# Attention scores over row halves of the array, the half-height mix first, and a projection spread over bank 7 and the next pair

## The reference, cut to what matters

```python
h = concat(patch_embedding(x), txt)                  # 8 x 178 x 192
xn = layernorm(layernorm(h)) * ln_w
Q = xn[:, None] * W_qk[None, :, None, :]             # 12 heads; queries are keys
attn = softmax(mask(Q @ Q^T / sqrt(192)))            # 178 x 178, causal
out = (attn @ (xn - mean(wte, axis=0))) / position   # wte: 50257 x 192
h = h + concat_heads(out) @ W_o.T                    # 2304 -> 192
h = h + experts(layernorm(h))                        # 16 experts and a shared one
```

## Time and profile before

| | |
|---|---|
| three runs | 474.68, 474.75, 476.51 us |
| the profiled execution | 476.25 us, its span 474.4 us |
| TensorE busy | 97% of the span |
| VectorE, ScalarE, GpSimd busy | 59%, 37%, 21% |
| attention, first scores to the end of the projections | about 18 to 278 us |
| transfers of wte | 26 to 220 us, at about 214 GB/s |
| TensorE's granted clock, mean | 0.989 |

### The profile page before, as it was taken

How to read it: one execution, slowest core, us unless ns; L and a number is a source line. 1 busy time by engine, 2 the same in 40 slices (tenths; PEclk the granted TensorE clock), 3 DMA queues, 4 the chain that set the end, 5 groups by cost and what they waited for, 6 DMA issues and landing times. The chain is left out here.

```text
span 474.4 us, 7317 instructions
## 1 busy us (share of the span) xinstructions
PE 459.4 (97%) x2692; PEld 397.7 (84%) x2692; DVE 281.9 (59%) x742; ACT 175.8 (37%) x573; POOL 101.8 (21%) x111
## 2 busy tenths in 40 slices
PE   8699999999999999999998999999999999999997
PEld 8387769866699666897766999989999999999996
DVE  7567856367572787507497636697447754754443
ACT  1365467044580555803445035532311231221211
POOL 6013122221223211210014014921170017000000
PEclk9799999999999999999899999999999999999999
DMA  7867999999999999978316023221323232223330
GB/s 206 255 241 138 213 214 211 214 215 212 214 214 213 214 213 213 214 151 213 120 37 240 2 72 69 61 48 65 86 63 61 66 80 61 63 73 72 74 66 25
DMA packets 23685, 64.99 MB, mean 137 GB/s; under 512 B 2876, under 2 KB 13332, under 8 KB 23266
## 3 DMA queue, kind: packets, MB, share of 16 engines
q0 software_dynamic: 7904, 40.86, 41.0%
q1 hardware_dynamic: 14882, 22.68, 17.6%
q10 hardware_dynamic: 864, 1.00, 0.6%
HBM read 61.88 MB, written 1.27 MB: 133 GB/s over the span
## 5 line engine op out<-in xcount | busy, mean ns | idle before, releaser
L513 ACT ACTIVATE pm<-bank,nmax 128x128 f32<-128x128 f32 x96 | 33.9, 365 | 106.0 <-DVE nmax L1011 106.0
L795 PE MATMUL bank<-woT,area_o 128*128 128x192 f32 (+1 forms) x432 | 71.4, 327 | 0.0
L1100 DVE TENSOR_TENSOR area_b<-area_b,area_w 128x356 f32<-128x356 f32 x64 | 33.9, 529 | 62.1 <-ACT area_b L581 62.0
L795 PEld LDWEIGHTS bank<-woT,area_o 128*128 128x128 f32 (+1 forms) x432 | 70.0, 182 | 0.4
L418 POOL DMA_DIRECT2D area_w<-in_L_attn_wte_dram x26 | 31.4, 1227 | 127.2 <-DMA area_w<-in_L_attn_wte_dram 127.2
L876 PE MATMUL bank<-area_w_r,area_o_r 128*128 128x356 f32 x112 | 43.9, 392 | 0.0
L742 PE MATMUL bank<-pT,xn 128*128 128x356 f32 x96 | 38.8, 486 | 1.1 <-issue 0.5
L581 ACT ACTIVATE area_b<-bank,area_k 128x356 f32<-128x356 f32 x32 | 17.8, 557 | 59.2 <-PE bank L880 59.1
L912 PE MATMUL bank<-area_k,area_b 128*128 128x192 f32 (+1 forms) x192 | 36.8, 327 | 0.0
L877 PE MATMUL bank<-area_w_r,area_o_r 128*128 128x356 f32 x112 | 36.4, 325 | 0.0
L539 ACT ACTIVATE area_b<-xb,w 64x192 f32<-64x192 f32 x96 | 34.5, 456 | 0.1
(11 more groups left out here) (219 smaller groups left out, 1012.9 us busy)
## 6 DMA issues: line engine op xcount, KB each, us to landing
area_w<-in_L_attn_wte_dram POOLq DMA_DIRECT2D x28, 1344.0 KB, 12.6
area_w<-gate_rows SPq DMA_DIRECT2D x64, 178.0 KB, 3.0
area_k<-in_experts_dram SPq DMA_DIRECT2D x8, 353.0 KB, 5.3
area_a<-in_experts_dram SPq DMA_DIRECT2D x6, 353.0 KB, 4.9
woT<-in_L_attn_W_o_dram SPq DMA_DIRECT2D x1, 1728.0 KB, 15.4
area_o<-in_x_dram SPq DMA_DIRECT2D x4, 384.0 KB, 9.1
area_w<-area_w POOLq DMA_DIRECT2D x1, 1344.0 KB, 9.8
area_b<-in_experts_dram SPq DMA_DIRECT2D x3, 353.0 KB, 7.0
```

Source lines behind the costliest of these rows:

```text
L513: last = act.activation(pm[:, sl, j, :], bank[0][:, j * P:(j + 1) * P], ACT.Exp, bias=nmax[:, sl, j:j + 1], accum_out=psums[:, sl, j:j + 1])
L795: last = pe.matmul(o, oT[:, c, at:at + n], woT[:, c, :], start=(c == 0), stop=(c == NCH - 1))
L1100: dve.tensor_tensor(sil[:, n % 2, :], sil[:, n % 2, :], wbc[:, m % RING, :], ALU.mult).then_inc(weighted, 1)
```

## The change

- **Scores.** Heads 0, 1 of a unit go to bank 0 and heads 2, 3 to bank 1, each bank holding the 256 columns of two heads and the 178 of their tail tile. The 64-row part is no longer padded: heads 0, 1 use partitions 0 to 63 and heads 2, 3 partitions 64 to 127, so that the two matmuls of such a step use the two row halves of the array and different banks. `xb` is kept twice, once in each half. The order is: 128-row parts of both banks, the masks, then the 64-row parts of the two banks, main and tail.
- **Behind the scores.** `maxima` is four reductions instead of two. The exponentials go bank by bank (two heads and a tail, then the other three); semaphores are one per bank instead of main and tail.
- **Start.** `xb` goes out of the bank twice (a second copy by ScalarE); the clearing of the padding by VectorE and GpSimd (L950, L405) is gone.
- **Mix.** The half-height part (bank 6) comes first, then banks 4 and 5; `mix_out` on VectorE takes bank 6 first.
- **Projection.** In pairs 0 to 2 tile 0 goes to bank 7 instead of bank 4. Tile 2 is left out at the end of the pair and comes in the next pair behind `scores(1)`; its residual moves along. In the last pair all three stay in order.

```diff
...
         emb_bank = [bank[n] for n in (6, 5, 4, 7)]
         in_a = area_a.shape[1] // WX
 
+        def projected(i, t):
+
+            if t == 2:
+                return bank[5][0:TT, 0:E]
+            return bank[7][:, 0:E] if t == 0 and i < PAIRS - 1 else bank[4][:, t * E:(t + 1) * E]
+
         def expert_at(e, plain):
 
             kept, a, b = (area_k, area_a, area_b) if plain else (round_k, round_a, round_b)
...
             pool.wait_ge(pool_own, own.at)
             pool.memset(wts[:], 1.0).then_inc(s_const, 1)
             pool.wait_ge(s_const, 1)
-            pool.memset(qb[64:P], 0.0).then_inc(s_pad, 1)
-            pool.wait_ge(s_pad, 3)
 
             def rstd(n, count):
 
...
 
                 act.wait_ge(xnT_psum, bt + 1)
                 act.activation(xa[:, b, :], bank[7][:, 0:SP], ACT.Copy).then_inc(xnT_ready, 1)
-                act.activation(xb[0:64, b, :], bank[7][0:64, SP:2 * SP], ACT.Copy).then_inc(xnT_ready, 1)
+                act.activation(xb[0:64, b, :], bank[7][0:64, SP:2 * SP], ACT.Copy)
+                act.activation(xb[64:P, b, :], bank[7][0:64, SP:2 * SP], ACT.Copy).then_inc(xnT_ready, 1)
 
             def exps(u, U):
                 sl = u % 2
-                act.wait_ge(max_main, U + 1)
-                for j in range(GRP):
-                    last = act.activation(pm[:, sl, j, :], bank[0][:, j * P:(j + 1) * P], ACT.Exp,
-                                          bias=nmax[:, sl, j:j + 1], accum_out=psums[:, sl, j:j + 1])
-                last.then_inc(exp_main, 1)
-                act.wait_ge(max_tail, U + 1)
                 for k in range(2):
-                    last = act.activation(pt[:, sl, k, :], bank[1][:, k * S:(k + 1) * S], ACT.Exp,
-                                          bias=nmax[:, sl, 4 + k:5 + k], accum_out=psums[:, sl, 4 + k:5 + k])
-                last.then_inc(exp_tail, 1)
+                    act.wait_ge(max_of[k], U + 1)
+                    for j in range(2):
+                        n = 2 * k + j
+                        act.activation(pm[:, sl, n, :], SIDE[k][:, j * P:(j + 1) * P], ACT.Exp,
+                                       bias=nmax[:, sl, n:n + 1], accum_out=psums[:, sl, n:n + 1])
+                    act.activation(pt[:, sl, k, :], SIDE_TAIL[k], ACT.Exp, bias=nmax[:, sl, 4 + k:5 + k],
+                                   accum_out=psums[:, sl, 4 + k:5 + k]).then_inc(exp_of[k], 1)
 
             def prob_out(u, U):
 
...
 
                 for g in groups:
                     for h in range(GRP * g, GRP * g + GRP):
-                        last = act.activation(qb[0:64, b, :, h, :], xb[0:64, b, :].rearrange("p (c t) -> p c t", c=3),
-                                              ACT.Copy, scale=w2b[:, h:h + 1])
+                        side = ROWS[h % GRP // 2]
+                        last = act.activation(qb[side, b, :, h, :], xb[side, b, :].rearrange("p (c t) -> p c t", c=3),
+                                              ACT.Copy, scale=w2b[side, h:h + 1])
                     last.then_inc(qb_ready, 1)
 
             turn_out(0, 0)
...
 
                 g, b = u % UPB, u // UPB
                 h = GRP * g
-                main = bank[0][:, :].rearrange("p (j t) -> p j t", j=GRP)
-                if not isinstance(U, int) or U:
-                    pe.wait_ge(exp_main, U)
-                split = bank[0][:, :].rearrange("p (j c t) -> p j c t", j=GRP, c=2)
-                pe.matmul(split, xa[:, b, 0:P], qa[:, b, 0:2, h:h + GRP, :].rearrange("p c j t -> p j c t"),
-                          start=True, stop=False)
-                pe.matmul(split, xb[:, b, 0:P], qb[:, b, 0:2, h:h + GRP, :].rearrange("p c j t -> p j c t"),
-                          start=False, stop=False)
-                pe.matmul(main, identb[:], cmask[:].rearrange("p (a t) -> p a t", a=1).broadcast_to([P, GRP, P]),
-                          start=False, stop=True).then_inc(scores_main, 1)
-                if not isinstance(U, int) or U:
-                    pe.wait_ge(exp_tail, U)
+                mains = [m.rearrange("p (j t) -> p j t", j=2) for m in SIDE]
+                splits = [m.rearrange("p (j c t) -> p j c t", j=2, c=2) for m in SIDE]
                 for k in range(2):
-                    o = bank[1][:, k * S:(k + 1) * S]
-                    pair_a = qa[:, b, 2, h + 2 * k:h + 2 * k + 2, :].rearrange("p j t -> p (j t)")
-                    pair_b = qb[:, b, 2, h + 2 * k:h + 2 * k + 2, :].rearrange("p j t -> p (j t)")
-                    pe.matmul(o, pair_a, xa[:, b, 0:S], start=(k == 0), stop=False, skip_group_check=True)
-                    pe.matmul(o, pair_b, xb[:, b, 0:S], start=False, stop=(k == 1), skip_group_check=True)
-                o = bank[1][:, 0:2 * S].rearrange("p (j t) -> p j t", j=2)[:, :, P:S]
-                pe.matmul(o, identb[:], tmask[:, 0:TAIL].rearrange("p (a t) -> p a t", a=1).broadcast_to([P, 2, TAIL]),
-                          start=False, stop=True, skip_group_check=True).then_inc(scores_tail, 1)
+                    at = slice(h + 2 * k, h + 2 * k + 2)
+                    if U:
+                        pe.wait_ge(exp_of[k], U)
+                    pe.matmul(splits[k], xa[:, b, 0:P], qa[:, b, 0:2, at, :].rearrange("p c j t -> p j c t"),
+                              start=True, stop=False, skip_group_check=True)
+                    pe.matmul(SIDE_TAIL[k], qa[:, b, 2, at, :].rearrange("p j t -> p (j t)"), xa[:, b, 0:S],
+                              start=False, stop=False, skip_group_check=True)
+                for k in range(2):
+                    pe.matmul(mains[k], identb[:], cmask[:].rearrange("p (a t) -> p a t", a=1).broadcast_to([P, 2, P]),
+                              start=False, stop=False, skip_group_check=True)
+                    pe.matmul(SIDE_TAIL[k][:, P:S], identb[:], tmask[:, 0:TAIL], start=False, stop=False,
+                              skip_group_check=True)
+                for k in range(2):
+                    at, side = slice(h + 2 * k, h + 2 * k + 2), ROWS[k]
+                    pe.matmul(splits[k], xb[side, b, 0:P], qb[side, b, 0:2, at, :].rearrange("p c j t -> p j c t"),
+                              start=False, stop=True, skip_group_check=True)
+                for k in range(2):
+                    at, side = slice(h + 2 * k, h + 2 * k + 2), ROWS[k]
+                    pe.matmul(SIDE_TAIL[k], qb[side, b, 2, at, :].rearrange("p j t -> p (j t)"), xb[side, b, 0:S],
+                              start=False, stop=True, skip_group_check=True).then_inc(scores_of[k], 1)
 
             def queries_in(bt, g):
 
...
                     pe.wait_ge(s_hin, 3)
                 if u % UPB == 0:
                     pe.wait_ge(xn_ready, 2 * i + b + 1)
-                for q in range(2):
-                    if u >= 1:
-                        if q == 0:
-                            pe.wait_ge(ot_act, U)
-                        else:
-                            pe.wait_ge(ot_dve, 2 * U)
-                    o = bank[4 + q][:, 0:2 * S].rearrange("p (j t) -> p j t", j=2)
-                    pe.matmul(o, xn[:, b, 0, 0:P], pT0[:, 2 * q:2 * q + 2, :], start=True, stop=True)
-                    pe.matmul(o[:, :, tl], xn[:, b, 1, 0:P], pT1[:, 2 * q:2 * q + 2, :], start=False,
-                              stop=True, skip_group_check=True).then_inc(pv_done, 1)
+                if U:
+                    pe.wait_ge(ot_dve, 2 * U - 1)
                 halves = [bank[6][64 * jj:64 * jj + 64, 0:2 * S].rearrange("p (q t) -> p q t", q=2) for jj in range(2)]
                 for jj, o in enumerate(halves):
                     pe.matmul(o, xn[:, b, 0, P:E], pT0[:, jj:GRP:2, :], start=True, stop=True)
...
                     last = pe.matmul(o[:, :, tl], xn[:, b, 1, P:E], pT1[:, jj:GRP:2, :], start=False,
                                      stop=True, skip_group_check=True)
                 last.then_inc(pv_done, 1)
+                for q in range(2):
+                    if U:
+                        pe.wait_ge(*((ot_act, U) if q == 0 else (ot_dve, 2 * U)))
+                    o = bank[4 + q][:, 0:2 * S].rearrange("p (j t) -> p j t", j=2)
+                    pe.matmul(o, xn[:, b, 0, 0:P], pT0[:, 2 * q:2 * q + 2, :], start=True, stop=True)
+                    pe.matmul(o[:, :, tl], xn[:, b, 1, 0:P], pT1[:, 2 * q:2 * q + 2, :], start=False,
+                              stop=True, skip_group_check=True).then_inc(pv_done, 1)
 
             def turn_a(i):
 
...
                     last = pe.transpose(bank[7][0:NW, at:at + n], wts[0:n, 3 * i + t, :], ident[0:n, 0:n])
                 last.then_inc(wT_psum, 1)
 
-            def project(U, last_pair=False):
-
-
-                pe.wait_ge(ot_act, U + UPP)
-                pe.wait_ge(ot_dve, 2 * (U + UPB))
-                for t, (at, n) in enumerate(COLS):
-                    if t == 1:
-                        pe.wait_ge(ot_dve, 2 * (U + UPP))
-                    o = bank[4][:, t * E:(t + 1) * E] if t < 2 else bank[5][0:TT, 0:E]
```

(73 more changed lines are left out.)

25 lines of the change are left out of this document (6 added, 19 removed).

## The result

The changed kernel takes **477.29 us** (median of 20 executions, 475.25 to 478.06) against 474.99 for the kernel before in the same comparison (20 executions, 473.77 to 479.86): ratio 1.0035, 95% interval 1.0019 to 1.0051. That is slower by a third of a per cent, inside the 0.5% called no change. The profiled execution took 476.07, with a span of 474.2 (before: 476.25 and 474.4). Executions of one kernel differ in their mean granted clock: in the three later comparisons the kernel before took 473.7 to 475.6 us at 0.992 or 0.993 (once 476.45) and 476.1 to 478.8 at 0.984 to 0.989.

The account below looks back on a forecast made before the run. TensorE paces the 24 units, but wte's folding transfer holds mean(): -1.9 - 0.5 - 0.4 + (4.0 - 1.7) = -0.5 from 476.25 gives 475.75; from the median, 475.95. Forecast 475.8 us, range 472.2 to 477.8.

Parts of the forecast that it names:

- rival 4: Clock stays down longer around mean(), a slow stretch as at the start: 475.8 + 1.6 = 477.4 us; chance 0.11.
- The unit: Steady attention unit on TensorE: scores 2.72 against 3.19 us, mix about -0.04; -0.5 in 19 units, -0.35 in 5.
- VectorE's stall: Four reductions cost VectorE +0.14 us a unit, yet no stall; other end 0.2 us in each of six heavy units.
- Projection: New tile placing removes three of four TensorE waits for the exponentials, 0.8 us gained; VectorE's residual wait changes nothing.
- Start: Extra copy before the first queries +0.2 us; -0.9 in all to the second scores' end; dropped clearing taken as 0.
- rival 2: Head start: VectorE, free of clearing, starts up to 1.8 us earlier, or slow stretch stays short: 471.5 to 472.4; chance 0.13.
- The fold: Folding transfer of wte lands 0.7 us earlier, at 219.1; mean() starts at 221.5, only 1.9 of 10 us gained.
- The hole: TensorE idle ahead of mean(), about from 212.5 to 221.5, about 9 us.
- The clock: Half rate from mean() into the scores of U = 21: loss 2.2 + 0.8 + about 1 = 4.0 us, instead of 1.7.
- Tail: Behind mean(): U = 21 gains 0.5 us; U = 22 and 23, paced by VectorE, gain 0.4 of TensorE's 0.46 wait.
- the first (the stage keeps its gain): Folding transfer not in the way, or stream gets faster: 10 + 0.5 + 0.4 us gained, about 464; chance 0.04.
- The third (serial halves): Row halves run one after the other: scores 3.45 us, +0.22 a unit, end at 479.5; chance 0.07.

Follow-up runs that it names:

- before_short: Kernel before the change with only 20 of the 28 transfers of wte, output short of the rest: 474.82 us, ratio 1.0002 to the kernel before.
- after_short: Changed kernel with only 20 of the 28 transfers of wte, output short of the rest: 464.68 us, ratio 0.9783 to the kernel before.
- after_nofold: Changed kernel with the folding transfer replaced by a VectorE addition and wte transfers 2 and 3 requested earlier: 466.83 us, ratio 0.9793 to the kernel before.
- short_same_half: Changed kernel with 20 of 28 wte transfers and both 64-row products in rows 0 to 63 of the array: 478.39 us, ratio 1.006.

## Why the prediction came out right

The account holds: a stage shorter by 10 us, of which the wait for the fold leaves 1 or 2 and the clock takes them. The time holds less well. The median, 477.29, is inside the range of 472.2 to 477.8, but 1.3 above the 475.95 that was worked out for it, 0.2 beyond the 477.1 that closed the forecast proper, and next to the 477.4 of rival 4, whose longer slow stretch the profiles do not show. The profiled execution, 476.07, fits its 475.75 well, in part by luck: the fold gave 0.6 less than taken, and the units behind `mean()` 0.5 more. Point by point:

- **The unit**, -0.5 predicted, -0.54 measured. The masks took 156.62 - 156.26 = 0.36 (0.37), the 64-row parts with a switch 0.94 (0.89). The Trainium skill's rule that a load goes by its columns, in "TensorE: Matmul & The Clock Gate", section "LDWEIGHTS (loading the stationary operand)", would have made the two passes of 178 columns 0.18 longer. The trace doesn't show that here: L706's group takes 0.40 with the switch behind it, and undoing the overlap costs the full 0.72, which leaves no room for the loads of the two halves having paced them. The same page of the Trainium skill has the rule that I should have set beside it, in "The mechanism": a load overlaps with running products where the row groups differ. The trace agrees, with the 0.72.
- **VectorE's stall**: none, as taken.
- **Projection**: the waits were gone as predicted, but the step was right for less than the whole reason. It priced the placing at the 0.8 that before showed and named the later exponentials; what it did not price is what they would have cost without it, 5.0.
- **Start**: the first scores began at 19.13 against 18.48, 0.65 later, where 0.2 was taken. The copy's step is 0.32 to 0.36 (L512 at 17.02, the queries at 17.38). The rest is mostly the clock: it was down to 0.56 from 15 to 16 already, before still full there, and from the first transpose to the first copy it was 1.37 (15.11 to 16.48) instead of 0.95. The clearing's gain of 0 was nearly right; the landing of the token bias and of the class tokens stands now where VectorE was held up:

```profile
7.70 0.36 DVE L968 TENSOR_TENSOR postab<-postab,tokb 128x192 f32<-128x192 f32 x1 [1.34 <-DMA tokb<-in_L_tok_b_dram]
...
9.80 0.62 DVE L1135 BATCH_NORM_STATS2 st<-hin 128x6 f32<-128x192 f32 x2 [1.75 <-DMA hin<-L_tok_cls_embedding_dram]
```

  Before, L1125, the same step, began at 10.02. So of the bound of 1.8 for rival 2, 0.2 came.
- **The fold**, the step with an error: GpSimd's second step came 1.0 earlier (0.7 predicted), but the fold only 0.14 (0.7). The next request went out at 47.25 (before 47.26), so the head start was lost within two transfers; why, no run shows. `mean()` gained 1.3 instead of 1.9. The prediction's reason, that the transfers run at the rate of the memory, isn't borne out: the first two transfers, which don't accumulate, ran at 425 to 430 GB/s from 30 to 34 in the kernel before, and the accumulating ones at about 215. What the sum needs, a stream that TensorE doesn't speed up, is what the runs show. GpSimd's second step now, and two stretches of before (columns as in the earlier trace rows):

```profile
35.14 1.04 POOL L415 TENSOR_TENSOR rs<-ve,mhalf 128x4 f32<-128x4 f32 x1 [8.57 <-DVE ve L989]
```

```profile
30.00:32.00 2.00, 2.00 (x15) 1.98 (x14) 0.51 (x2) 1.86 (x11) 0.00 (x0) 1.00 1.00 425
...
44.00:46.00 2.00, 2.00 (x12) 1.58 (x11) 1.52 (x4) 0.88 (x5) 0.00 (x0) 1.00 1.05 215
```

- **The hole**: from 212.2 to 222.1, 9.9 us (about 9 predicted).
- **The clock**: by half of the slow stretch 4.0 us in place of 1.7, as worked out. Step by step it is a little less, and split otherwise: `mean()` 4.04 - 2.26 = 1.8 (2.2 predicted), the transposes 227.92 - 226.16 = 1.76 in place of 0.93, 0.8 as predicted, and the scores half of 230.2 - 227.92, 1.1 (about 1).
- **Tail**: the expected 0.4 of the earlier trace rows did not come there. That wait shrank from 0.46 to 0.37, and two others grew: 0.46 (L691) from 0.25, and 0.57 (L745) from 0.46. The last projection began 0.4 earlier all the same (259.80 against 260.20). With 1.3 gained at `mean()` and 2.3 lost by the clock, the units between must have given 1.4, where 0.9 was taken.
- **The median**: I took it that the kernel before has no slow stretch at `mean()` in its median execution. Its executions bear that out: they are of two kinds (0.992 or 0.993, and 0.984 to 0.989), and the profiled one is of the second. So does the profile of before_short, which has 0.993 and the full clock through `mean()`. The changed kernel has 0.980 at best, and both its profiles have the slow stretch. Its own median lies 1.2 above its profiled execution; eleven of its twenty executions have a clock of 0.974 or less instead of 0.977, and an estimate of 0.003 x 475 is 1.4 us. In which stretch those lose it, no profile shows. This is the part of the median that the sum lacked.
- **The range**: two of its rivals were placed wrongly by their own sums. For rival 2, a head start of 1.8 alone gives 475.95 - 1.8 = 474.2, and a short slow stretch alone 475.95 - 2.3 = 473.7, both inside the forecast; only the two together reach 471.9. Rival 4's 477.4 is inside the range too, and was counted as slower than it.

Of the rivals, the first (the stage keeps its gain) is what after_short and after_nofold measured, 464.7 and 466.8, once the stream or the fold was out of the way. The third (serial halves) is excluded by short_same_half.

## What to carry to other kernels

Before a stage is made faster, look for the next thing that the stage ends in and that isn't driven by it: here the margin against a transfer was 1.2 us, and the change brought 10. Then the shortening and the removal of that transfer are one change, each worth nothing alone (0 and 0) and about 8 to 10 us together (after_nofold against the kernel before, with two transfers requested earlier besides). And read what a part of a change is worth inside the change, not against the kernel before: the placing of the projection showed 0.8 there and was worth 5.0.

## What the runs showed of the hardware

- Two fp32 products of 64 rows, in different halves of the array's rows and in different banks, overlap fully: 0.94 us for both pairs of parts, 1.66 in one half.
- After 9.3 us of matmuls of 192 columns and a wait of 1.8, `mean()` (products of one column) ran at full clock, and the clock fell behind it (0.58 from 226 to 230). Where TensorE had no long wait ahead of `mean()`, it fell in some profiles (after_short, 0.72 from 216 to 222) and not in others (before_short, 1.00 from 222 to 230). At the lower level, 1.2 GHz, `mean()` took 4.04 instead of 2.26.
- A transfer from one half of a tile of the on-chip memory to the other, with an addition, took 9.8 us for 1344 KB from issue to landing (10.1 to 10.9 in four other executions); VectorE adds the same in 2.94.
- The small operation of VectorE that in the earlier trace rows took 2.10 and ended with GpSimd's clearing takes 0.36 without it (L968).
